# Wider queue rows in a routed expert layer: the scaled row and the residual are stored by GpSimd instead of being rebuilt when a row is read back

## The reference, cut to what matters

```python
x  = layernorm(x + attention(x))                    # 128 values, no scale and shift here
mu, var = mean(x), mean((x - mu) ** 2)
xn = (x - mu) * rsqrt(var + 1e-5) * gamma + beta    # what the router and the experts read
probs = softmax(xn @ router_w.T / 1.5)              # 8 experts
w, idx = top_k(probs, 2)
y = sum(w[k] * (silu(xn @ W1[idx[k]]) @ W2[idx[k]]) for k in range(2))
out = layernorm(y + 2 * x)
```

## Time and profile before

| | |
|---|---|
| median of 3 runs | 1298.41 us (1298.08 to 1298.52) |
| the profiled execution | 1298.3 us; its span 1296.6 us |
| PE busy | 1273.5 us, 98% of the span |
| PEld busy | 1129.2 us, 87% |
| DVE busy | 1094.0 us, 84% |
| ACT busy | 1158.6 us, 89% |
| POOL busy | 748.4 us, 58% |
| granted TensorE clock, mean | 0.996 of full speed |
| attention part | from the start to about 988 us |
| expert part | about 988 to 1252 us; the rest is the final layer norm |

### The profile page before, as it was taken

How to read it: one execution, slowest core, us unless ns; L and a number is a source line. 1 busy time by engine, 2 the same in 40 slices (tenths; PEclk the granted TensorE clock), 3 DMA queues, 4 the chain that set the end, 5 groups by cost and what they waited for, 6 DMA issues and landing times.

```text
span 1296.6 us, 36408 instructions
## 1 busy us (share of the span) xinstructions
PE 1273.5 (98%) x11106; PEld 1129.2 (87%) x11106; DVE 1094.0 (84%) x5167; ACT 1158.6 (89%) x3655; POOL 748.4 (58%) x1333
## 2 busy tenths in 40 slices
PE   7999999999999999999999999999998999999997
PEld 6888888888888888888888888888887999999993
DVE  6888888888888888888888888888897798788857
ACT  7999999999989998899899999899886999999957
POOL 2346666666555655556656655555556676555545
PEclk9999999999999999999999999999998999999999
DMA  5000000000000000000000000000032232222229
GB/s 210 6 14 22 23 22 23 23 24 28 19 14 15 14 14 14 14 14 14 14 14 14 15 14 16 16 21 17 14 144 91 69 89 84 76 78 78 69 82 339
DMA packets 49215, 60.98 MB, mean 47 GB/s; under 512 B 8304, under 2 KB 35059, under 8 KB 48768
## 3 DMA queue, kind: packets, MB, share of 16 engines
q1 hardware_dynamic: 39376, 41.44, 9.9%
q0 software_dynamic: 8640, 17.13, 3.9%
q10 hardware_dynamic: 1008, 0.08, 0.1%
HBM read 30.72 MB, written 28.81 MB: 46 GB/s over the span
## 4 chain that ended last, share of the span: by engine, by line
PE 91%; ACT 4%; DVE 1%; issue 1%; DMA 1%; POOL 0%; ACTq 0%; SPq 0%; POOLq 0%; DVEq 0%
PE ps_a L1261 15%; PE ps_s L1304 13%; PE ps_s L1283 11%; PE ps_b L1296 7%; PE ps_f L1339 7%; PE ps_s L1261 7%; PE ps_f L1296 6%; PE ps_b L1555 4%; PE ps_s L1286 4%; PE ps_a L1555 4%; PE ps_b L1261 4%; PE ps_f L1261 3%; PE ps_s L1620 2%; PE ps_a L1360 1%; ACT f_y L682 1%
## 5 line engine op out<-in xcount | busy, mean ns | idle before, releaser
L682 ACT ACTIVATE f_y<-f_y,neg_max 128x256 f32<-128x256 f32 x512 | 256.5, 501 | 45.6 <-DVE neg_max L962 45.6
L962 DVE CUSTOM_DVE_ANT_0 f_y<-ps_s,mask 128x256 f32<-128x256 f32 x512 | 214.6, 419 | 62.3 <-PE ps_s L1286 62.0
L1261 PE MATMUL ps_a<-xt_hi,weights 128*128 128x256 f32 x1024 | 241.5, 299 | 0.0
L581 POOL TENSOR_TENSOR ot_lo<-f_y,ot_hi 128x512 fp32r<-128x512 f32 x128 | 164.9, 1288 | 115.9 <-PE ps_s L1286 110.6
L978 DVE TENSOR_SCALAR f_y<-f_y,inv_sums 128x256 f32<-128x256 f32 x512 | 194.6, 380 | 7.0
L685 ACT ACTIVATE f_y<-f_y,neg_max 128x128 f32<-128x128 f32 x512 | 200.0, 391 | 0.0
L1304 PE MATMUL ps_s<-ident,f_y 128*128 128x128 f32 x1536 | 196.6, 275 | 0.0
L647 POOL DMA_INDIRECT y_tok<-f_y,m_dest x142 | 140.2, 987 | 88.7 <-DVE m_dest L1167 61.1
L1261 PEld LDWEIGHTS ps_a<-xt_hi,weights 128*128 128x128 f32 x1024 | 175.5, 189 | 16.0 <-issue 10.8
L1283 PE MATMUL ps_s<-qk 64*128 64x256 f32 x1024 | 176.5, 421 | 5.1 <-ACT pt L730 2.3
L1304 PEld LDWEIGHTS ps_s<-ident,f_y 128*128 128x128 f32 x1536 | 172.9, 142 | 5.1 <-issue 0.5
(11 more groups left out here) (227 smaller groups left out, 3467.6 us busy)
## 6 DMA issues: line engine op xcount, KB each, us to landing
m_x<-queue SPq DMA_DIRECT2D x71, 133.0 KB, 2.3
f_y<-y_tok SPq DMA_DIRECT2D x32, 256.0 KB, 6.4
queue<-empty SPq DMA_DIRECT2D x8, 532.0 KB, 3.6
x_raw<-in_x SPq DMA_DIRECT2D x32, 128.0 KB
out_x<-f_y SPq DMA_DIRECT2D x16, 256.0 KB, 6.7
y_tok<-f_y,m_dest POOLq DMA_INDIRECT x142
f_y<-in_w SPq DMA_DIRECT2D x1, 2048.0 KB, 10.9
m_w<-in_w SPq DMA_DIRECT2D x1, 2048.0 KB, 14.8
```

What stands on the lines that cost most here:

```text
L581: pool.tensor_tensor(ot_lo[:, first:first + 2, :], ot[:, s % 2], ot_hi[:, first:first + 2, :].bitcast(F32), ALU.subtract).then_inc(ot_lo_d ...
L682: act.activation(row[:, 0:2 * P], row[:, 0:2 * P], ACT.Exp, scale=-1.0, bias=neg_max[:, pair, h, 0:1], accum_out=sums[:, d % 2, pair, h, 0:1])
L962: dve.tensor_tensor_reduce(out=row[:, 0:2 * P], in0=ps_s[:, pair, h, 0:2 * P], in1=mask[:].rearrange("p a b -> p (a b)"), scale=-1.0, scal ...
L1261: ins = pe.matmul(dst, lhs, rhs, start=(i == 0), stop=(i == len(terms) - 1))
```

## The change

Queue rows grow from 133 to 260 words: 128 of xn with gamma and beta applied, 128 of the residual (once in each of the two rows), TOK, SLOT, GATE, MORE. KEEP and all that formed and used it are gone. POOL makes the rows in a function of its own, `make_lines(n - 1)`, placed behind its work of the third step. DVE's `residual(n)` now waits for `lines_done` of the sequence before instead of `z_done`. In the expert part ACT only rounds the transposed rows, DVE subtracts from PSUM and adds the residual straight from the loaded rows; a load waits for the output rows (`m_rows_done`) of the buffer's last use, with five buffers instead of four. `slots(SEQS)` moves behind iteration 0's output, its sends to iterations 2, 4, 6 and 8; `make_lines(SEQS)` runs at iteration 10, `slots(SEQS + 1)` at 11, its sends at 13, 15, 17 and 19. At the start, `empty` is filled behind the other constants, and two broadcast loads of gamma and beta rows are added on SP.

```diff
-WBUFS = 4
+WBUFS = 5
-    LINE = D + 5
-    TOK, SLOT, GATE, MORE, KEEP = D, D + 1, D + 2, D + 3, D + 4
+    LINE = 2 * D + 4
+    TOK, SLOT, GATE, MORE = range(2 * D, LINE)
...
-        z = sb("z", [P, 2, TILES, LINE])
+        z = sb("z", [P, TILES, D])
+        line = sb("line", [P, 2, TILES, LINE])
...
-        m_x = sb("m_x", [P, WBUFS, BLOCKS, LINE])
+        m_x = early_use[:, 0:WBUFS * BLOCKS * LINE].rearrange("p (a b d) -> p a b d", a=WBUFS, b=BLOCKS)
...
-            sp.wait_ge(consts_ready, 1)
+            for dst, src in ((gamma_row, gamma), (beta_row, beta)):
+                sp.dma_start(dst[:], src.rearrange("p o -> o p").to_broadcast([P, D])).then_inc(rows_loaded, 16)
+            sp.wait_ge(empty_ready, 1)
...
                 if j >= WBUFS:
-                    sp.wait_ge(m_xt_ready, j - WBUFS + 1)
-                    sp.wait_ge(m_gate_done, j - WBUFS + 1)
-                    sp.wait_ge(m_keep_done, j - WBUFS + 1)
+                    sp.wait_ge(m_rows_done, j - WBUFS + 1)
...
             def norm(n):
...
-                if n >= 3:
-                    pool.wait_ge(tokens_sent[par], (n - 1 - par) * (TILES * TOP * 8))
-                pool.tensor_tensor(z[:, par, :, TOK], z[:, par, :, TOK], two_seqs[:], ALU.add)
...
                 ins.then_inc(z_done, 1)
-                pool.tensor_tensor(ln_r1[:], ln_a[:], neg_half[:, 0:TILES], ALU.pow).then_inc(ln_link, 1)
-                pool.tensor_tensor(ln_br[:], ln_b[:], ln_r12[:], ALU.mult).then_inc(ln_link, 1)
-                pool.wait_ge(ln_link, link(6))
-                pool.tensor_tensor(ln_r1neg[:], ln_r1[:], neg_two[:], ALU.mult).then_inc(ln_link, 1)
-                pool.wait_ge(ln_link, link(8))
-                pool.tensor_tensor(z[:, par, :, KEEP], ln_br[:], ln_r1neg[:], ALU.mult).then_inc(keep_done, 1)
+            def make_lines(n):
+                link = lambda k: (n - 1) * LINE_LINKS + k
+                par = (n - 1) % 2
+                rows = line[:, par, :, 0:D]
+                pool.tensor_tensor(ln_r1[:], ln_a[:], neg_half[:, 0:TILES], ALU.pow).then_inc(line_link, 1)
+                pool.wait_ge(z_done, n)
+                if n == 1:
+                    pool.wait_ge(rows_loaded, 16 * 2)
+                if n >= 3:
+                    pool.wait_ge(tokens_sent[par], (n - 1 - par) * (TILES * TOP * 8))
+                pool.tensor_tensor(rows, z[:], gamma_row[:].unsqueeze(1).to_broadcast([P, TILES, D]), ALU.mult
+                                   ).then_inc(line_link, 1)
+                pool.wait_ge(line_link, link(1))
+                pool.tensor_tensor(ln_shift_half[:], ln_negmean[:], ln_r1[:], ALU.mult).then_inc(line_link, 1)
+                pool.tensor_tensor(line[:, par, :, TOK], line[:, par, :, TOK], two_seqs[:], ALU.add)
+                pool.wait_ge(line_link, link(2))
+                pool.tensor_tensor(rows, rows, beta_row[:].unsqueeze(1).to_broadcast([P, TILES, D]), ALU.add)
+                pool.wait_ge(line_link, link(3))
+                for i in range(TILES):
+                    ins = pool.tensor_scalar(line[:, par, i, D:2 * D], res[:, i, :], ln_r1[:, i:i + 1],
+                                             ln_shift_half[:, i:i + 1], ALU.mult, ALU.add)
+                ins.then_inc(lines_done, 1)
...
             def step(n, q, d):
...
                 if q == 1 and n - 1 in LATE:
                     send_tokens(n - 1, 1)
+                if q == 2 and n in LATE:
+                    make_lines(n - 1)
...
             send_tokens(SEQS - 1, 1)
+            make_lines(SEQS - 1)
             norm(SEQS)
-            slots(SEQS)
-            for i in range(TILES):
-                send_tokens(SEQS, i)
...
-                if j == 9:
+                if j in (2, 4, 6, 8):
+                    send_choice(SEQS, (j // 2 - 1) // TOP, (j // 2 - 1) % TOP)
+                if j == 10:
+                    make_lines(SEQS)
+                if j == 11:
                     slots(SEQS + 1)
-                    for i in range(TILES):
-                        send_tokens(SEQS + 1, i)
+                if j in (13, 15, 17, 19):
+                    send_choice(SEQS + 1, (j - 13) // 2 // TOP, (j - 13) // 2 % TOP)
...
+                if j == 0:
+                    slots(SEQS)
...
-            def affine(j):
+            def round_x(j):
                 act.wait_ge(m_xt_ready, j + 1)
                 if j >= 2:
-                    act.wait_ge(m_xlo_done, j - 1)
                     act.wait_ge(m_z_ready, (j - 1) * 2)
-                act.activation(m_xf[:, j % 2, :], ps_a[:, 0, 0:ROWS], ACT.Identity, scale=gamma_sb[:, 0:1],
-                               bias=beta_sb[:, 0:1]).then_inc(m_xnt_done, 1)
-                act.wait_ge(m_xnt_done, j + 1)
-                act.activation(m_xhi[:, j % 2, :], m_xf[:, j % 2, :], ACT.Copy).then_inc(m_xhi_done, 1)
+                act.activation(m_xhi[:, j % 2, :], ps_a[:, 0, 0:ROWS], ACT.Copy).then_inc(m_xhi_done, 1)
...
-                keep(j)
...
             def residual(n):
...
                 if n >= 2:
-                    dve.wait_ge(z_done, n - 1)
+                    dve.wait_ge(lines_done, n - 1)
...
-                dve.tensor_tensor(m_xlo[:, j % 2, :], m_xf[:, j % 2, :], m_xhi[:, j % 2, :].bitcast(F32), ALU.subtract
+                dve.tensor_tensor(m_xlo[:, j % 2, :], ps_a[:, 0, 0:ROWS], m_xhi[:, j % 2, :].bitcast(F32), ALU.subtract
...
                 if j >= 1:
-                    pe.wait_ge(m_xnt_done, j)
+                    pe.wait_ge(m_xlo_done, j)
```

100 lines of the change are left out of this document (42 added, 58 removed).

## The result

The changed kernel takes 1302.83 us (median of 6 runs, 1302.20 to 1303.82) against 1298.24 us of the kernel before (6 runs): ratio 1.0032, 95% interval 1.0022 to 1.0043. That is 4.6 us slower; 9.7 were forecast. The profiled execution took 1302.2 us, with a span of 1300.5 against 1296.6, 3.9 us more.

What follows compares the result with a forecast made beforehand. PE was taken to pace the attention part, and PE, then ACT, the expert part. Terms of 5.8 + 5.0 + 1.5 - 2.6 = +9.7 us on 1298.3 gave 1308.0 us, range 1295.5 to 1316.

Steps and rivals of the forecast that it cites:

- second rival: Whole kernel: near zero, one of two collisions at half price, the other absorbed; 1298 to 1299 us, chance 0.13.
- What bounds the kernel: PE paces the attention part, 30.55 us per sequence; expert iterations go at PE's pace, later at ACT's, 0.045 us slower.
- Third step: Attention part: DVE scales blocked beside `make_lines` delay the residual and what follows, 0.18 us in 28 sequences: +5.0 us.
- third rival: Attention part: POOL waits for DVE's scales, so `make_lines` ends late and the residual waits; 1314 us, chance 0.10.
- Fourth step: Attention part: POOL's cast, now earlier, blocks DVE's scales and delays PE's scores, 0.20 us in 29 sequences: +5.8 us.
- Ends of the attention part: Doubled DMAs of `empty` slow two or three further queue sends, mostly hidden by POOL's idle time: +1.5 us once.
- Expert part: Expert iterations: less ACT work, spread sends and earlier output rows, against a longer first load: together -2.6 us.
- the router's iteration: Expert part, where the router's ranks are formed: spreading late sends removes POOL's backlog, -1.9 us.
- the 1.0: Expert part: ACT loses 1.35 us per iteration, so 23 iterations fall to PE's pace, -1.0 us.
- the transposes wait for DVE: Expert part: PE's next transposes wait for DVE's subtraction instead of ACT's first read, showing at most at the start: +0.2 us.
- rival of absorption: Attention part keeps 30.55 us per sequence because idle time hides both collisions; only the expert part counts: 1295.7 us, chance 0.17.

Runs made afterwards that it cites:

- lines_longer: The changed kernel with one more multiplication of 256 elements (0.74 us) ahead of the first operation of `make_lines`: 1320.24 us in one execution.
- cast_held: The changed kernel, but POOL's first cast of a sequence waits until DVE's last scale of the sequence before is done: 1299.49 us, ratio 1.0006.
- before_long: The kernel before the change with queue rows of 260 words instead of 133, the added words zero: 1300.03 us, ratio 1.0016.
- table_spread: The changed kernel with the six parts of DVE's second table moved from iterations 10 to 15 to every fifth from 10 to 35: 1301.49 us, ratio 1.0019.
- send_aside: Held cast, spread table, last queue sends at 24 to 39, plus one indirect send at iteration 60 to an unused region; against the kernel before: 1297.13 us, ratio 0.9988.

## Why the prediction was right or wrong

The sign was right and the range held the time, but the amount was twice too large, and the sign came by luck, since two errors hide each other. In the profiled executions all that comes ahead of the last landing adds up to -0.95 us, where the forecast has +9.7, and the DRAIN, which it does not have, adds 4.8. Without the DRAIN the changed kernel would be within what a measurement can tell from no change: by its own mechanisms the forecast should have ended near its second rival.

- **What bounds the kernel:** right. 30.55 us per sequence and the expert part's waits are where the trace after differs.
- **Third step, +5.0 taken (0 to 12):** the step that failed. The collision came, one per sequence at 0.48 us and not two, and `make_lines` was costed right (3.47 against 3.54 us from its start). But the 0.41 us of idle time and the 0.08 us by which the residual starts ahead of the copy's recorded end took all of it; 0 reached PE in 29 sequences, and only in the one from 30 to 31 did a wait of 0.79 us. I had let "a part" remain where the rows gave a comparison: one blocked scale of 0.48 us against 0.41 and a copy that overlaps. lines_longer shows how near the edge that is: the third rival is real from 0.1 us on.
- **Fourth step, +5.8 taken (0 to 7):** right mechanism, both forms of it, wrong size: 2.3. The distance from L736 to the scores grew by 0.24 or 0.15 us, as in the earlier trace rows, but the period by 0.12 or 0.03; PE makes up 0.12 before it waits again. I took a distance within a step for a loss per sequence. cast_held shows that the term is the fourth step's alone.
- **Ends of the attention part, +1.5:** the stretch with the DMAs of `empty` grew by 1.1, but not because they doubled: before_long doubles them and adds nothing. It is `make_lines` at two scales, with PE's wait of 0.79, and the cast (0.4). The term rests on a misreading of the earlier trace rows: the 1.93 us are not the price of a send beside these DMAs. After the change the 114th send waits 1.78, and the three others of the sequence, beside the same DMAs, 0.17 to 0.31. The -1.0 of the next stretch is scatter.
- **Expert part, -2.6:** the router's iteration fell from 5.50 to 3.65 us as forecast (-1.9). From iteration 20 on 2.5 us went, more than the 1.0: ACT's pace is gone, and PE's own is 3.420 and not 3.446. That the transposes wait for DVE was costed at +0.2 "at most at the start". It cost 0.8 net against before and 1.4 by table_spread: I had asked only if DVE has time on average, and not what else stands in its queue in iterations 10 to 15.
- **Not in the forecast:** POOL's last DRAIN, +4.8. Before the change it ended 2 us ahead of the program's end, so no view of waits or of the chain named it; only the rows of the closing line do. What the change does to POOL's queue was followed to its last send and no further.
- The rival of absorption had the third step and the expert part right, and the third rival's mechanism (DVE holding up `make_lines`) costs POOL 0.2 us (L513 at 0.89 instead of 0.69) and no more.

## What to carry to other kernels

An operation moved to an engine that has time can still cost the neighbour that shares its port, and only at the places where that neighbour's slack is smaller than one blocked instruction: read the slack at each place, and hold the cheap operation back with a semaphore (here 1.9 us for one wait). Where a wait changes from one engine to another, look for the stretch in which the new engine does other work. And look at what ends the program behind the last useful instruction: a DRAIN that was hidden can become the longest single loss.

## What the runs showed of the hardware

- POOL's closing DRAIN grew by 0.0817 us for each indirect DMA issued since the last regular queue send: 4.75, 5.56, 8.01, 8.83, 8.99 and 9.32 us for 54, 64, 94, 104, 106 and 110 sends, though the last of them was sent 35 us earlier, yet 1.64 us for 124 in the old order. There rows of 133 or 260 words make no difference (1642 and 1643 ns).
- Ahead of the program's 114th indirect DMA POOL paused for 1.50 to 1.93 us in all nineteen kernels, with no semaphore to wait for; in the old order it paused again, for 2.16 us, ahead of the 114th behind the last queue send.
- A DVE `tensor_scalar` of 128 or 256 elements beside POOL's cast, addition or multiplication took 0.65 to 0.83 us instead of 0.28 to 0.35. Which of the two waits can't be read from the starts: a scale recorded 0.03 us ahead of the cast took 0.72 us in one form and 0.28 in the other, where POOL's cast took 0.72 instead of 0.61.
- The pace of an expert iteration changed between kernels whose PE work is the same: 3.446 before, 3.427 in before_long, 3.420 after, and 3.446 again in send_aside, which has one small tile and one send more. The cause was not tried; tiles at other addresses are one possibility.
